# The index columns of two gather stages: copied by ScalarE many groups ahead, not by GpSimd one group ahead

## The reference

```python
# layer 0, attention over edges (4 heads of 64)
h = (x @ W).reshape(N, H, C)
e = jax.nn.leaky_relu(a_src[src] + a_dst[dst], NEG_SLOPE)
alpha = softmax of e over the edges of each destination
out = jax.ops.segment_sum(h[src] * alpha[:, :, None], dst, num_segments=N)
# layer 1, messages of an edge network
w = silu(edge_scalars @ fc_w1 / sqrt(8)) * SILU_NORM @ fc_w2 / sqrt(64)
xg0 = y0[edge_src]; xg1 = y1[edge_src]
mids = products of w, xg0, xg1 and edge_attr (512 numbers for each edge)
agg = jax.ops.segment_sum(mids, edge_dst, num_segments=n)
```

## Time and profile before

| | us |
| --- | --- |
| median of 3 runs | 3763.07 (3760.01 to 3765.9) |
| span of the profiled execution | 3834.3 |
| TensorE busy | 3096.8 (81%) |
| VectorE busy | 2264.0 (59%) |
| GpSimd busy | 1887.1 (49%) |
| ScalarE busy | 1426.5 (37%) |

### The profile page before, as it was taken

One profiled execution on the slowest core, in us unless ns is written; L12 is line 12 of the kernel. 1 busy time (PEld: TensorE's weight loads), 2 busy tenths in 40 slices (PEclk: granted clock), 3 DMA queues, 4 the chain that ended last, 5 costly groups with the idle time before them and its releaser, 6 DMA issues. The chain is left out here.

```text
span 3834.3 us, 80836 instructions
## 1 busy us (share of the span) xinstructions
PE 3096.8 (81%) x22728; PEld 2335.4 (61%) x22728; DVE 2264.0 (59%) x6165; ACT 1426.5 (37%) x4367; POOL 1887.1 (49%) x2266
## 2 busy tenths in 40 slices
PE   6577777777777768789996888888888888878499
PEld 4466666666666666578884545555554545548388
DVE  5455565555555557756665656566666656666712
ACT  5122222222222216623332444454444544417322
POOL 3566666666666641111114566666665555541144
PEclk9788888888888889999997989898889998989699
DMA  6433333333333336533223333333333323325321
GB/s 194 125 93 89 92 92 90 92 91 90 92 90 94 97 89 179 167 98 91 83 75 94 89 88 91 90 91 92 91 90 90 87 80 88 97 75 170 113 53 48
DMA packets 239108, 375.94 MB, mean 98 GB/s; under 512 B 88190, under 2 KB 145606, under 8 KB 238762
## 3 DMA queue, kind: packets, MB, share of 16 engines
q0 software_dynamic: 89712, 230.26, 21.7%
q1 hardware_dynamic: 147482, 140.83, 13.2%
q10 hardware_dynamic: 1696, 2.62, 0.2%
HBM read 310.75 MB, written 62.84 MB: 97 GB/s over the span
## 5 line engine op out<-in xcount | busy, mean ns | idle before, releaser
L1990 POOL DMA_INDIRECT e_rows<-tab,e_ix x828 | 785.3, 948 | 447.1 <-issue 333.0
L588 POOL DMA_INDIRECT e_rows<-tab,e_ix x830 | 789.1, 951 | 345.2 <-issue 302.8
L983 PE MATMUL e_pU<-e_ohp,e_rows 128*128 128x128 f32 x3340 | 516.0, 321 | 17.6 <-issue 13.6
L983 PEld LDWEIGHTS e_pU<-e_ohp,e_rows 128*128 128x128 f32 x3340 | 499.9, 237 | 26.9 <-issue 21.0
L2232 PE MATMUL e_pU<-e_msg,e_oh 128*32 128x128 f32 (+1 forms) x6672 | 427.9, 326 | 40.8 <-issue 34.8
L2162 DVE TENSOR_TENSOR e_msg<-e_pW,e_rows 128x256 f32<-128x256 f32 x417 | 176.5, 423 | 457.9 <-remote 251.5
L2164 DVE TENSOR_TENSOR e_msg<-e_pW,e_rows 128x384 f32<-128x384 f32 x834 | 422.2, 548 | 0.0
L697 ACT CAST e_ohT<-e_pT 64x640 bf16<-64x640 f32 x167 | 114.4, 685 | 825.1 <-remote 451.3
L2218 PE MATMUL e_pW<-e_w,e_hT 64*128 64x256 f32 x1668 | 340.9, 459 | 71.8 <-DVE e_msg L2164 24.3
L2232 PEld LDWEIGHTS e_pU<-e_msg,e_oh 128*32 128x32 f32 x6672 | 263.0, 117 | 194.0 <-issue 135.4
L964 PE MATMUL e_pT<-ident,e_oh 128*64 128x128 f32 x835 | 152.1, 321 | 185.5 <-issue 95.4
(11 more groups left out here) (453 smaller groups left out, 5669.7 us busy)
## 6 DMA issues: line engine op xcount, KB each, us to landing
e_rows<-tab,e_ix POOLq DMA_INDIRECT x1658
xnT<-f_xnT SPq DMA_DIRECT2D x25, 250.0 KB, 3.0
e_xk<-xnT SPq DMA_DIRECT2D x25, 250.0 KB
xnT<-b_xT SPq DMA_DIRECT2D x25, 250.0 KB, 2.9
m_xnT<-xnT SPq DMA_DIRECT2D x25, 250.0 KB
xnT<-m_xT SPq DMA_DIRECT2D x25, 250.0 KB, 2.7
ffn_norm<-xnT SPq DMA_DIRECT2D x25, 250.0 KB
tab<-f_hrow SPq DMA_DIRECT2D x25, 227.5 KB
```

Source lines behind the costliest of these rows:

```text
L588: nc.gpsimd.indirect_dma_start(out=rows[:, s, j, :], out_offset=None, in_=env["tab0"], in_offset=bass.IndirectOffsetOnAxis(ap=at[:, j:j + ...
L983: nc.tensor.matmul(pU[:, s % 2, 2 * W * k:2 * W * (k + 1)], rows[:, s, j, 128 * k:128 * k + 128], ohp[:, s % 3, j, 2 * k:2 * k + 2, :], st ...
L1990: nc.gpsimd.indirect_dma_start(out=rows[:, r % PER, j, :], out_offset=None, in_=env["tab1"], in_offset=bass.IndirectOffsetOnAxis(ap=at[:, ...
```

## The change

`ix` becomes a ring of six groups in the first stage and of ten in the second. GpSimd makes no copy. ScalarE makes them: in the first stage after the exp of group g the columns of g + 6, into the slot that g had, in all steps below `LATE` (156 copies); in the second between the copy of the sums and the silu of step g the columns of g + 9, in steps 1 to 125 (125 copies). In the loops GpSimd waits for the copy of its own group (`s_ix`, from g - 5 and g - 9 on); in the groups written out before and after the loops it reads its columns straight from `srcI`, at a fixed address, and waits for none. The copies for groups behind the loops are made and not read.

```diff
@@ edges0
-        ix = sb("ix", [P, 2, GT], I32)
+        ix = sb("ix", [P, SLOTS, GT], I32)
@@ edges0, gpsimd
-                        at = ix[:, s % 2, :] if lo >= 1 else srcI[:, 0:GT]
-                        if lo >= 1:
-                            pool.wait_ge(s_ix, g)
+                        at = ix[:, s, :] if k is not None else srcI[:, g * GT:g * GT + GT]
+                        if k is not None:
+                            pool.wait_ge(s_ix, g - SLOTS + 1)
@@
-                            if j == 3 and hi <= GROUPS - 2:
-                                nc.gpsimd.tensor_copy(ix[:, (s + 1) % 2, :], srcI[:, bass.ds((g + 1) * GT, GT)])\
-                                  .then_inc(s_ix, 1)
@@ edges0, scalar
                         nc.scalar.activation(p[:, s % 3, :, 0:H0], ee[:, 4 + s % 2, :, :], ACT.Exp).then_inc(s_p, 1)
+                        if hi < LATE:
+                            nc.scalar.copy(ix[:, s, :], srcI[:, bass.ds((g + SLOTS) * GT, GT)]).then_inc(s_ix, 1)
@@ edges1
-        ix = sb("ix", [P, 2, T1], I32)
+        ix = sb("ix", [P, 2 * PER, T1], I32)
@@ edges1, gpsimd
-                        at = ix[:, r % 2, :] if lo >= 1 else srcI[:, 0:T1]
-                        if lo >= 1:
-                            pool.wait_ge(s_ix, g)
+                        at = ix[:, r, :] if lo < hi else srcI[:, g * T1:g * T1 + T1]
+                        if lo < hi:
+                            pool.wait_ge(s_ix, g - 2 * PER + 1)
@@
-                            if j == 3 and hi <= GROUPS1 - 2:
-                                nc.gpsimd.tensor_copy(ix[:, (r + 1) % 2, :], srcI[:, bass.ds((g + 1) * T1, T1)])\
-                                  .then_inc(s_ix, 1)
@@ edges1, scalar
                             copied(g - 1, lo - 1)
+                        if lo >= 1 and hi <= LAST:
+                            nc.scalar.copy(ix[:, (r - 1) % (2 * PER), :], srcI[:, bass.ds((g + 2 * PER - 1) * T1, T1)])\
+                              .then_inc(s_ix, 1)
                         if hi <= GROUPS1 - 2:
                             silu(g + 1, r + 1, lo + 1)
```

## The result

The changed kernel takes 3717.56 us (median of 4 runs, 3714.76 to 3720.15; in the experiments this version is called after), the kernel before, run beside it, 3761.54 (4 runs, 3752.89 to 3765.9). The ratio is 0.9889, 95% interval 0.9876 to 0.9901: **44 us faster**. The forecast was no change (3765.0), its range 3745 to 3786; of its rivals the first, with a chance of 0.08, came nearest (GpSimd's gathers pace both stages, 3705).

A forecast was written before the change was run, and what follows sets the result against it. TensorE, VectorE and ScalarE were taken to pace most of both stages, GpSimd only their starts: 3834.3 - 1.0 - 3.2 + 2.3 + 3.8 = 3836.2 us, less the 71.2 us span-to-median difference, 3765.0; range 3745 to 3786.

The forecast's parts named there:

- The reading of who leads: Both edge stages: TensorE, VectorE and ScalarE pace each other and GpSimd's gathers follow, except at each stage's start.
- rival 1: GpSimd paces all of both stages; dropping its copies gives (166 + 138) x 0.19 = 58 us, 3705; chance 0.08.
- the difference is carried over as it is: Whole kernel: median 3763.07 lies 71.2 us below the profiled span 3834.3; kept constant, turning 3836.2 into 3765.0 us.
- GpSimd paces about 5 and 17 groups only: At the starts of the first and second stage; removing copies there saves 1.0 and 3.2 us, together 4.2.
- ring leads of 2.2 and 4 groups: Gathers issued ahead of VectorE's use, at 1000 us (first stage) and 3200 us (second); taken to show GpSimd follows.
- The wait behind the copy: GpSimd's copy behind a landing wait delays the next gather; priced at 0.19 us a group where GpSimd paces.
- ScalarE's terms: Copies at 0.15 us each delay the first stage's square, 2.3 us, and the second's silu, 3.8 us.
- the second stage's two terms: Second stage: 3.2 us less from GpSimd's copies removed, 3.8 us more from ScalarE's copies before the silu.
- rival 2: Second stage: ScalarE's copy makes the silu late in every group, 125 x 0.26 = 32.5 us, 3794; chance 0.09.
- Rival 2's extreme form: Second stage: ScalarE's integer copy calls for a table load, 125 x 1.28 = 160 us, 3923; chance 0.01.
- rival 3: First stage: GpSimd's copies held up VectorE's e_ee; freed, 0.068 x 166 = 11.3 us less there, 3754; chance 0.06.
- 19.5 as its far bound: Whole kernel: largest slowdown the unknown costs alone allow, reaching from -6.7 to +19.5 us, 3756 to 3783.

The follow-up runs named there:

- again2: The kernel before, unchanged, profiled for a third trace, on another chip than A: 3833.25 us.
- A: One of four chips, not a run; the kernel before has medians of 3756.57 and 3755.26 us on it.
- again: The kernel before, unchanged, profiled once more on A: 3755.75 us.
- act4: The changed kernel with three more ScalarE copies in front of each of its index copies, both stages, on A: 3716.28 us, 0.9898 to the kernel before.
- D: One of four chips, not a run; the kernel before has a median of 3815.92 us on it.
- only0: The kernel before with the change in the first edge stage only, on A: 3733.71 us, 0.9939.
- C: One of four chips, not a run; the kernel before has a median of 3876.3 us on it.
- after2: The changed kernel once more, on C: 3914.61 us, 1.0093 to the kernel before.
- twice: The kernel before with a second GpSimd copy in front of each index copy: 3773.04 us, 1.0042 on A; repeated on D 3820.67 us, 1.0005.

## Why the prediction was wrong

**The reading of who leads** was right for its trace and wrong for the kernel as it was timed. Counts, slot waits and stage ends do describe that execution, and again2 repeats it. On A, and in the runs that timed the change, the gathers pace all the way, the case of rival 1.

**The step that failed** is "the difference is carried over as it is". A span 71.2 us above the median was taken for a constant. It was the sign that the profiled execution ran another way: its first stage took 1309.6 us and 1271.2 in again, its second 1379.7 and 1368.2, with TensorE held up in its matmuls. The trace had rows on that, one for a line of each stage, which the reading passed over:

```profile
PE e_pE L973 <- issue: 73.0, 82, 2.0
...
PE e_pU L2232 <- issue: 34.8, 77, 1.1
```

L973 is the logits of the first stage, L2232 the sums of the second. Counted over all of TensorE's lines, and only at matmuls that carry no wait and follow one of the same line and tiles, such idle time comes 123 times in the first stage of that trace (80.7 us) and 93 times in the second (39.6 us); in again and in after it doesn't come once. What the runs showed in place of the carried-over difference: without it the users of the rows keep up, and GpSimd's gathers pace both stages from end to end. The steps before it, that GpSimd paces about 5 and 17 groups only and that 4.2 us come of it, fall with that. Before the sum came the question whether an execution without those 71 us would still be paced by the users. With ring leads of 2.2 and 4 groups built from a small difference in rate, the answer was open, and rival 1 deserved far more than 0.08.

**The wait behind the copy**, 0.19 us a group: measured 0.14 and 0.16 us, in all 304 groups and not in 22. The 0.19 came from single rows of a timeline (a gap of 1.52 us with the copy, 1.26 and 1.35 without); the medians of that same trace are 1.47 and 1.45 us with it, and those of the changed kernel 1.36 and 1.32 without. By rival 1's 0.19 the sum was 58 us, by the measured ones it is 45.3, and 44 came out.

**ScalarE's terms**, 2.3 and 3.8 us: nothing on A. With the gathers pacing, VectorE's e_ss never waits for the square, before or after the change, where the earlier trace rows had 30 waits, and TensorE's e_pW waits for the silu 3 times before and 2 after, where the earlier trace rows had 25. The copy's price was set too high as well: it lasts 0.181 and 0.195 us, but what stands behind it starts 0.097 us after it in act4, where the sum had 0.15. The estimate of 0.10 us from the Trainium skill's figures ("ScalarE: Activation LUTs", What ACT_TABLE_LOAD costs) agrees with that. On D, where users pace, the second stage's two terms together (-3.2 + 3.8 = 0.6 us) agree with 1.0018 (0.9997 to 1.0039), but that interval reaches from 1 us less to 15 us more and tests neither term.

**Rivals 2 and 3** fall on A: act4 had four copies, some 0.38 us, in front of the silu, 1.5 times rival 2's 0.26, and lost nothing; both before and after the change ScalarE loads a table 207 times. (Rival 2's extreme form was also added up wrong: 3923 is the median and 160 us alone, with the rival's own 30.6 us it is 3954.) VectorE's e_ee operation takes 0.179 us in the middle with GpSimd's copies (again) and without (after), and the rare long one isn't theirs: 0.254 us at most in only0 and 0.222 in act4, whose first stages have no copy on GpSimd. Of the 14 that took over 0.19 us in the prediction's trace one ran beside a copy of GpSimd (0.215 us). The rule that rival 3 took from the Trainium skill ("SBUF — State Buffer", Who interferes with whom) had next to nothing to act on: in again no e_ee operation ran beside a copy, in again2 two did, at 0.179 and 0.180 us.

**What the forecast would have been on C** is wrong too, on the other side: 1.0093 is 36 us (23 at least by the interval) where it had 1.9, with 19.5 as its far bound. There the users' own pace fell. In the second stage of after2 42 of 138 groups take over 11 us from first gather to next first gather, in again2 3, in the first trace of before 13; on D 17 with the change in this stage and 3 with twice. The other groups take 9.53 to 9.57 us with the change and 9.68 to 9.74 without (9.74 with twice's two copies). So the gathers do go faster in most groups, and more groups then wait for a slot. On D that cancels; on C it more than cancels, and why it does isn't settled: no trace of before on C was taken, and only0 wasn't run there.

## What to carry to other kernels

Compare the profiled execution's span with the spread of the timed runs before anything else. If it lies outside by more than the effect looked for, the trace may show another regime, or another chip: work out the sum for both, "this engine paces" and "it follows", and weigh them by how small the lead is that the trace shows. Idle time that is put down to "issue" in the middle of a run of matmuls is such a sign. And a small operation behind a wait costs the step from the wait to it, so moving it ahead of the wait gives most of what removing it gives (29 of 44 us here, on A).

## What the runs showed that was not expected

- The same kernel takes 3755 to 3876 us on the four chips, and the size and even the sign of an edit go with it: the change 0.9889 and 1.0093, the older landing waits 0.8932 and 1.116 to 1.1221. A version that is 10.7% faster on A is no better kernel for the others.
- A landing wait between gathers makes a gap of 1.27 to 1.38 us in place of 0.30, once a group in the first stage and twice in the second; the older waits took 176 and 210 us off the two stages on A and brought the whole time 361 us below the changed kernel's, eight times what the change did.
- A second small copy right behind a first on GpSimd costs 0.058 us, though its duration is 0.18; the gather behind a copy takes 0.97 us in place of 0.945.
- 843 more copies on ScalarE moved the time on A by less than can be told. With the change alone it is busy 404 of 1340 and 724 of 1410 us in the two stages, and a copy that lasts 0.18 us puts off what stands behind it by 0.097.
